# A two-layer graph network on one core: gathers, pair sums and loads placed in the time in which the first table is cleared

## The reference

```
h   = x mapped by lin1, times node_vec1            # 64 scalars, 32 vectors
w   = silu(edge_attr_64 @ fc_w1) @ fc_w2           # per-edge weights
es, ev = h_s[src], h_v[src]                        # gather of the source's row
m   = products of w, es, ev and edge_attr_4 (scalar, vector and cross products)
agg = segment_sum(m, dst)                          # scatter with addition
x1  = layernorm(x + gated(self_connection(x) + lin2(agg)))
```

## Time and profile before

| | us |
|---|---|
| median of 3 runs (lowest, highest) | 2219.08 (2218.88, 2225.33) |
| the profiled execution, its own time | 2213.97 |
| its span in the trace | 2212.2 |
| first layer, edges: start to the last scatter's landing | 0 to 767.7 |
| of that, up to the first scatter | 119.5 |
| first layer, nodes | to about 1170 |
| second layer, edges, with its start | to about 1920 |
| second layer, nodes | to 2212.2 |

### The profile page before, as it was taken

How to read it: one execution, slowest core, us unless ns; L and a number is a source line. 1 busy time by engine, 2 the same in 40 slices (tenths; PEclk the granted TensorE clock), 3 DMA queues, 4 the chain that set the end, 5 groups by cost and what they waited for, 6 DMA issues and landing times.

```text
span 2212.2 us, 47355 instructions
## 1 busy us (share of the span) xinstructions
PE 1427.5 (65%) x10302; PEld 1309.2 (59%) x10302; DVE 1478.8 (67%) x5824; ACT 1079.7 (49%) x3532; POOL 1507.3 (68%) x2020
## 2 busy tenths in 40 slices
PE   2098888888888566666655998888888888100000
PEld 2087777777777366566554987888888888000000
DVE  3087777777777188888883766555565565188886
ACT  1054444444444157767775545444454454066666
POOL 3067888778787456666664677777777776388876
PEclk7599999999999788999987999999999999555555
DMA  9956666666666578888874776676766776599996
GB/s 388 405 109 139 135 139 135 135 136 134 132 137 145 106 215 260 266 263 267 265 238 148 167 170 159 156 154 155 156 153 162 155 161 132 132 330 354 353 356 251
DMA packets 267990, 439.88 MB, mean 199 GB/s; under 512 B 34992, under 2 KB 145264, under 8 KB 264688
## 3 DMA queue, kind: packets, MB, share of 16 engines
q1 hardware_dynamic: 164400, 306.89, 43.2%
q0 software_dynamic: 75264, 67.79, 22.1%
q10 hardware_dynamic: 28224, 64.24, 7.7%
HBM read 235.50 MB, written 203.27 MB: 198 GB/s over the span
## 4 chain that ended last, share of the span: by engine, by line
POOL 28%; DMA 22%; issue 19%; PE 13%; DVE 6%; ACT 5%; SPq 4%; ACTq 1%; POOLq 0%; DVEq 0%
POOL table L459 13%; DMA table<-sums,row_all 9%; DMA tab<-table 7%; POOL xg L442 7%; DMA xg<-x_rows,src_all 3%; POOL half_rstd L495 3%; SPq L348 3%; DVE res L991 3%; ACT y L788 3%; DMA attrT<-in_attrT 3%; DVE stats L1000 2%; PE ps L590 1%; POOL gate L517 1%; PE ps L628 1%; PE ps L576 1%
## 5 line engine op out<-in xcount | busy, mean ns | idle before, releaser
L459 POOL DMA_INDIRECT table<-sums,row_all x392 | 631.3, 1610 | 351.5 <-ACT sums L742 161.8
L788 ACT ACTIVATE y<-res,shift,rstd 128x160 f32<-128x160 f32 x784 | 343.1, 508 | 233.4 <-POOL rstd L498 193.5
L727 ACT COPY msg<-ps 128x192 f32<-128x192 f32 (+1 forms) x196 | 57.4, 293 | 546.1 <-PE ps L609 541.0
L442 POOL DMA_INDIRECT xg<-in_x_rows,src_all x196 | 201.9, 1030 | 59.6 <-issue 58.4
L442 POOL DMA_INDIRECT xg<-x_rows,src_all x196 | 195.6, 998 | 68.2 <-issue 58.8
L934 DVE SCALAR_TENSOR_TENSOR x1g<-ps,a_all,x1g 128x160 f32<-128x160 f32 x392 | 132.5, 379 | 151.5 <-PE ps L629 151.2
L1000 DVE BATCH_NORM_STATS2 stats<-res 128x6 f32<-128x160 f32 x784 | 195.6, 311 | 4.6
L853 DVE TENSOR_TENSOR prod<-hs,ea_all 128x192 f32<-128x192 f32 x196 | 69.9, 357 | 190.2 <-ACT hs L702 187.9
L889 DVE TENSOR_TENSOR pe<-ps,ea_all 128x192 f32<-128x192 f32 x196 | 70.1, 358 | 166.6 <-ACT msg L727 134.0
L495 POOL TENSOR_TENSOR half_rstd<-var,minus_half 128x8 f32<-128x8 f32 x98 | 167.3, 1707 | 14.0
L590 PE MATMUL ps<-weights,midT 128*128 128x128 f32 (+1 forms) x784 | 165.4, 295 | 15.4 <-DVE msg L894 15.0
(11 more groups left out here) (114 smaller groups left out, 4782.0 us busy)
## 6 DMA issues: line engine op xcount, KB each, us to landing
tab<-table SPq DMA_DIRECT2D x98, 384.0 KB, 3.8
table<-zeros SPq DMA_DIRECT2D x24, 1536.0 KB, 37.4
table<-zeros SPq DMA_DIRECT2D x98, 324.0 KB
tab<-table SPq DMA_DIRECT2D x98, 324.0 KB, 5.1
x_rows<-y ACTq DMA_DIRECT2D x98, 320.0 KB, 3.1
x1g<-x_rows SPq DMA_DIRECT2D x98, 320.0 KB
base_rows<-x1g SPq DMA_DIRECT2D x98, 320.0 KB, 2.7
x1g<-base_rows SPq DMA_DIRECT2D x98, 320.0 KB, 4.8
```

Of the source, the lines that this page charges most:

```text
L442: pool.indirect_dma_start(out=xg[j % RING][:, t, 0:width], out_offset=None, in_=rows, in_offset=bass.IndirectOffsetOnAxis(ap=src_all[:, at ...
L459: pool.indirect_dma_start(out=table[l], out_offset=bass.IndirectOffsetOnAxis(ap=row_all[:, at:at + 1], axis=0), in_=sums[j % 4][:, t, 0:W] ...
L788: last = nc.scalar.activation(y[u][:, t, :], res[u][:, t, :], ACT.Identity, scale=rstd[u][:, t:t + 1], bias=shift[u][:, t:t + 1])
```

## The change

GpSimd's list in the first layer's edge part becomes: gathers of pairs 0 to 41, scatters of pairs 0 to 29, then in turn gather j+12 and scatter j for j = 30 to 85, then scatters 86 to 97. The gathers of pairs 0 to 33 (`EARLY`) write into the memory of `x1g` and `tab`, those of 34 to 41 into the eight `xg` buffers. A gather from pair 8 on waits, among the first 42, only until the gather of eight pairs before has landed. The sums of pairs 0 to 18 (`EARLY_SUMS`) are put into the memory of `res` and `y`, so that ScalarE needn't wait for a scatter before pair 23. The loads of edge scalars and destinations get rings of eight. SP issues eight of the 25 clearing DMAs behind the loads of pair 7 and the other 17 between the loads of pairs 8 to 19, one and two in turn; the clearing of the second table trails by 26 steps in place of 8. The first 34 steps are written out on each engine, in place of 10. The second layer changes only in its larger rings.

```diff
+EARLY, EARLY_SUMS = 34, 19
+AHEAD, BURST = EARLY + 8, 30
...
-        attrT = four("attrT", [P, P])
-        dst_row = four("dst_row", [P, PAIR], I32)
+        attrT = eight("attrT", [P, P])
+        dst_row = eight("dst_row", [P, PAIR], I32)
...
+        early_xg = (parts(x1g_all[:, :, :, :].rearrange("p u t c -> p (u t c)"), D + 1) +
+                    parts(tab_all[:, :, :, :].rearrange("p h g c -> p (h g c)"), D + 1))
+        early_sums = (parts(res_all[:, :, :, :].rearrange("p u t c -> p (u t c)"), 192) +
+                      parts(y_all[:, :, :, :].rearrange("p u t c -> p (u t c)"), 192))
...
                 def load_attr(j, m, u):
 
-                    wait_count(sp, s_hid, j - 3)
+                    wait_count(sp, s_hid, j - 7)
...
                 def load_dst_row(j, m, u):
 
-                    wait_count(sp, s_same, j - 3)
+                    wait_count(sp, s_same, j - 7)
...
                 def clear_table0(j, m, u):
-                    if isinstance(m, int) and m == 3:
+
+                    if not isinstance(m, int) or not RING - 1 <= m < EARLY:
+                        return
+                    if m == RING - 1:
                         sp.wait_ge(s_fill, 1)
...
+                    done = 0 if m == RING - 1 else RING + (m - RING) * 3 // 2
+                    for k in range(done, min(25, RING + (m - RING + 1) * 3 // 2)):
...
-                run_stages(sp, base, NP, 10, [(0, load_attr), (0, load_dst_row)] +
-                           ([(0, clear_table0), (8, clear_table1)] if l == 0 else [(4, store_base), (0, load_x1)]), RING)
+                run_stages(sp, base, NP, 10 if l else 26, [(0, load_attr), (0, load_dst_row)] +
+                           ([(0, clear_table0), (26, clear_table1)] if l == 0 else [(4, store_base), (0, load_x1)]), RING, 10 if l else EARLY)
...
                 def gather(j):
 
-                    wait_count(pool, s_xgT, j - RING + 1)
-                    if l == 0:
-                        wait_count(pool, s_ea, j - RING + 1)
+                    if l == 1 or j >= AHEAD:
+                        wait_count(pool, s_xgT, j - RING + 1)
+                        if l == 0:
+                            pool.wait_ge(s_ea, j - RING + 1)
+                    elif j >= RING:
+                        pool.wait_ge(s_gather[j % RING], landed(j - RING, j % RING, RING, 32))
...
-                for k in range(l * NP, (l + 1) * NP + RING):
-                    if k < (l + 1) * NP:
-                        gather(k)
-                    if k - RING >= l * NP:
-                        scatter(k - RING)
+                first, last = l * NP, (l + 1) * NP
+                ahead, burst = (RING, 0) if l else (AHEAD, BURST)
+                for j in range(first, first + ahead):
+                    gather(j)
+                for j in range(first, first + burst):
+                    scatter(j)
+                for j in range(first + burst, last):
+                    if j - burst + ahead < last:
+                        gather(j - burst + ahead)
+                    scatter(j)
...
                 def copy_sums(j, m, u):
 
                     act.wait_ge(s_sum, j + 1)
-                    wait_count(act, s_scat[u % 4], landed(j - 4, u % 4, 4, 32))
-                    copy(sums[u][:, :, 0:W], sum_ps[l][:, :, :]).then_inc(s_sumsb, 1)
+                    if not (isinstance(j, int) and j < EARLY_SUMS + 4):
+                        act.wait_ge(s_scat[u % 4], landed(j - 4, u % 4, 4, 32))
+                    copy(sums_of(j, u)[:, :, 0:W], sum_ps[l][:, :, :]).then_inc(s_sumsb, 1)
```

More of the change, by code:

```diff
@@ L53, in wait_count, with run_stages @@
         eng.wait_ge(sem, n)
-def run_stages(eng, base, count, depth, stages, unroll=4):
-    assert (count - depth) % unroll == 0
-    for k in range(base, base + depth):
+def run_stages(eng, base, count, depth, stages, unroll=4, lead=None):
+    lead = lead or depth
+    assert (count - lead) % unroll == 0
+    for k in range(base, base + lead):
         for lag, f in stages:
@@ L179, in program @@
         zT = four("zT", [T * V, P])
-        x1g = eight("x1g", [P, T, D])
+        x1g_all = sb("x1g", [P, RING, T, D])
+        x1g = [x1g_all[:, u, :, :] for u in range(RING)]
         x1z = two("x1z", [P, T, V])
         z1T = four("z1T", [P, 2, P])
-        tab2 = [sb(f"tab{h}", [P, 2, T * 192]) for h in range(RING // 2)]
+        tab_all = sb("tab", [P, RING // 2, 2, T * 192])
+        tab2 = [tab_all[:, h, :, :] for h in range(RING // 2)]
         tab = [tab2[u // 2][:, u % 2, :].rearrange("p (t c) -> p t c", t=T) for u in range(RING)]
         gate = two("gate", [P, T, 96])
-        res = eight("res", [P, T, D])
+        res_all = sb("res", [P, RING, T, D])
+        res = [res_all[:, u, :, :] for u in range(RING)]
         stats2 = [sb(f"stats{h}", [P, 2, T, 6]) for h in range(RING // 2)]
@@ L194, in program, with parts, xg_of, sums_of @@
         shift = [shift2[u // 2][:, u % 2 * T:(u % 2 + 1) * T] for u in range(RING)]
-        y = four("y", [P, T, D])
+        y_all = sb("y", [P, 4, T, D])
+        y = [y_all[:, u % 4, :, :] for u in range(RING)]
+        def parts(flat, width):
+            n = flat.shape[1] // (2 * width)
+            cut = flat[:, 0:n * 2 * width].rearrange("p (n t c) -> p n t c", n=n, t=2)
+            return [cut[:, k, :, :] for k in range(n)]
+        early_xg = (parts(x1g_all[:, :, :, :].rearrange("p u t c -> p (u t c)"), D + 1) +
+                    parts(tab_all[:, :, :, :].rearrange("p h g c -> p (h g c)"), D + 1))
+        early_sums = (parts(res_all[:, :, :, :].rearrange("p u t c -> p (u t c)"), 192) +
+                      parts(y_all[:, :, :, :].rearrange("p u t c -> p (u t c)"), 192))
+        assert len(early_xg) >= EARLY and len(early_sums) >= EARLY_SUMS
+        def xg_of(j, u):
+            return early_xg[j] if isinstance(j, int) and j < EARLY else xg[u]
+        def sums_of(j, u):
+            return early_sums[j] if isinstance(j, int) and j < EARLY_SUMS else sums[u % 4]
         small2 = [sb(f"small{h}", [P, 4, 2, T]) for h in range(RING // 2)]
@@ L235, in program @@
         s_src = sem("src_loaded")
-        s_attr = sem4("attr_loaded")
-        s_drow = sem4("dst_row_loaded")
+        s_attr = [sem(f"attr_loaded{u}") for u in range(RING)]
+        s_drow = [sem(f"dst_row_loaded{u}") for u in range(RING)]
         s_gather = [sem(f"rows_gathered{u}") for u in range(RING)]
@@ L442, in gather @@
                         pool.indirect_dma_start(
-                            out=xg[j % RING][:, t, 0:width], out_offset=None, in_=rows,
+                            out=xg_of(j, j % RING)[:, t, 0:width], out_offset=None, in_=rows,
                             in_offset=bass.IndirectOffsetOnAxis(ap=src_all[:, at:at + 1], axis=0)).then_inc(s_gather[j % RING], 16)
@@ L806, in _ @@
             nc.vector.memset(zeros[:, :], 0.0).then_inc(s_fill, 1)
+            for u in range(RING):
+                nc.vector.memset(attr1T[u][:, :], 0.0)
             for u in range(4):
-                nc.vector.memset(attr1T[u][:, :], 0.0)
                 nc.vector.memset(z1T[u][:, :, :], 0.0)
```

33 lines of the change are left out of this document (16 added, 17 removed).

## The result

The changed kernel takes 2239.93 us (2238.43 to 2245.53, 5 runs) beside 2219.08 us (2213.70 to 2225.33, 5 runs) for the kernel before: the ratio is 1.0097, with a 95% interval of 1.0077 to 1.0117. It is about 21 us slower, where 3 us less had been forecast, and outside the range. The profiled executions have spans of 2238.1 and 2212.2 us; these are 25.9 us apart and not 21, as the profiled execution before lies 5 us under the median.

The account below looks back on a forecast made before the run. It took full DMA to bound the edge part up to the first scatter, then GpSimd's loop, with scatter landings just underneath. A start 10.1 us later minus 12.9 us of faster scatters gave -2.8 us: 2216.3 us, range 2203 to 2231.

Parts of the forecast that it names:

- The loop at 6.62: First layer's edge part: 56 scatter intervals with gathers keep 6.62 us each, 370.7 us; SP's longer lag costs zero.
- the second limit: Edge loop: each scatter waits for the previous landing, so removing two gathers saves only 0.23 to 0.5 us a period.
- The start: First layer's scatter 0: starts at 129.6 us instead of 119.49, losing 10.1 us, behind the clearing and gather 41.
- Gathers: Under the clearing: 27 more pairs landed, 0.43 us each, delay its end by 11.6 us (9.9 to 15.6).
- Loads: Ahead of the last clearing DMA: sixteen more pairs at 0.57 us, 9.1 us, plus 1 us for SP's issue.
- The gathers' landing: Gathers ahead of scatter 0: at most 3.38 us a pair, so gather 41 is out at 126.2.
- rival B: Gathers become the bound at 4.1 us a pair; scatter 0 at 142, total 2228.7 us; chance 0.21.
- bare periods: Scatters without gathers between them: 29 intervals at 6.3 us each, 182.7 us together.
- the last twelve: Final bare scatter intervals up to scatter 97: 25.6 us, 8.3 over a clearing burst, and 42.7.
- Rival A: Clearing hardly pays for loads and gathers, ending near 122; 16 to 18 us faster, 2202; chance 0.29.
- Rival C: Bare scatters no faster, landing stretched to 3.1 us by loads and pieces; 2224 us; chance 0.13 with Rival D.
- Rival D: List misbehaves, for instance TensorE held back after its rest, loop 30 to 85 slower; 5 us and more, counted in Rival C.

Follow-up runs that it names:

- a_sync: The changed kernel, but in SP's written loop the second table's clearing piece waits for scatter k-12 instead of k-26; 2222.89 us, ratio 1.0036 to the kernel before.
- v_gather: v_eight with the changed kernel's 42 pairs of gathers ahead and 30 scatters in a row; 2214.49 us, ratio 0.9990 to the kernel before.
- v_eight: The kernel before with load rings of eight and the first table's whole clearing behind pair 7's loads instead of pair 3's; 2209.30 us, ratio 0.9959.
- v_eight_again: The same kernel as v_eight, timed in more rounds on another occasion, against the kernel before; 2210.56 us, ratio 0.9955.
- v_six: v_eight with the first table's clearing behind pair 5's loads instead of pair 7's; 2207.53 us, ratio 0.9947 to the kernel before.
- b_nogather: The kernel before without the first layer's gathers from pair 8 on, so results are wrong; loop period 6.35 us instead of 6.64, one run 2194.47 us.
- v_lag26: v_eight with the second table's clearing piece waiting for scatter k-26 instead of k-8, 34 SP steps written out; 2291.51 us, ratio 1.0373.
- v_lag26_noclear: v_lag26 with the second table's clearing pieces moved into one burst behind the last loads; loop period 7.03 us, total 2289.45 us.
- b_noclear1: The kernel before with the second table's clearing pieces moved into one burst behind the last loads; loop period 6.54 us instead of 6.64, one run 2253.52 us.

## Why the prediction was wrong

*The loop at 6.62, wrong.* This is the step that failed outright: 18.4 of the 21.4 us that the pace was short of the forecast. The prediction looked at SP's longer lag only for whether loads would come too late, and put "zero". They came early enough; what the lag took away was the moment of issue. With SP held by landings (a_sync, v_gather) the loop is 6.61 and 6.58. That the landing was the second limit, 0.23 us under the loop, stood two paragraphs earlier, and so did the share of pieces and loads in the traffic; what was missing was that anything which moves those transfers against the scatter moves the period.

*The start, mis-sized in two terms.* Scatter 0 came 137.15 - 107.6 = 29.6 us behind the mark of the kernel before, where 21.7 had been forecast for the clearing. Gathers: 0.43 us a pair was right (0.45 and 0.46), but all 33 more pairs went inside the clearing, not 27: 14.9 us in place of 11.6. (The prediction's upper case and the expectation of v_gather count 34.)

Loads: the rest, 14.6 us in place of 9.1 + 1. It is 3.7 us for the first four pairs (v_eight, 111.34 - 107.6; 3.3 by v_eight_again), and 10.9 us between v_gather and after. For the second part here are packets and SP's queue, first of v_gather from 122 us to its scatter 0 and from 0 to 122, then of after from 133 us to its scatter 0 and from 0 to 133:

```profile
DMA packets 534, 0.74 MB, mean 174 GB/s; under 512 B 125, under 2 KB 440, under 8 KB 534
...
q1 hardware_dynamic: 6603, 42.31, 84.8%
```

```profile
DMA packets 756, 0.60 MB, mean 145 GB/s; under 512 B 84, under 2 KB 742, under 8 KB 756
...
q1 hardware_dynamic: 10936, 45.33, 85.5%
```

Behind 122 and 133 us every packet is under 8 KB, so the clearing's rows of 12 KB are all through. Up to these marks, 11 us apart, SP's queue moved 3.02 MB more in after. At 0.197 MB a pair of loads that is about 15 pairs, not 12, and its packets took 113.7 - 103.5 = 10.2 us more: 0.67 us a pair, just within the prediction's bound of 0.68. So two things were missed. The middle of 0.46 and 0.68 was taken, and the loads of some three pairs that stand behind the last clearing piece in SP's list were carried ahead of its last rows, so a load that is written behind the clearing isn't always transferred behind it. From 130 us to scatter 0, only nine of 1681 packets are of 8 KB or more: this is the thin tail. It isn't after's own cost, since in v_gather, too, the last 4.2 us ahead of scatter 0 have no row of the clearing. From 133 us on after moves loads alone, 0.60 MB with 54.6% of 4.15 us: 0.74 us a pair, so the excess over their bytes' 0.46 does not need the clearing beside them. The 0.92 us a pair that the expectation of v_six works with counts twelve pairs where fifteen went.

*The gathers' landing, wrong.* Rows of the first three pairs were read as a pace of 3.38 us; GpSimd issued all 84 gathers at 1.25 us with no wait, the last at 108.90, and scatter 0 waited 27.31 us for the clearing alone. So rival B had the right sign for the wrong reason. The rule that the Trainium skill gives in "DMA: Bandwidth & Descriptors", section "Queues, rings and completion order" (queues take turns packet by packet), was applied with four packets of a gather per engine, which gave 4.1 us a pair. The trace of after holds 4032 packets on GpSimd's queue for 84 gathers, three per gather and engine if all engines have the same share, which by that rule is an estimate of 2.8 us a pair with 0.46 us per clearing packet. At an issue of 2.5 us no gather had to wait for the one of eight pairs before, which allows for a lag, so no run here tells whether the rule held them.

```profile
q0 software_dynamic: 4032, 6.93, 14.1%
```

*Right:* bare periods (6.38 for 6.3), the last twelve (77.3 for 76.6), the second limit (b_nogather 6.35), TensorE's rest without harm, no effect on the later parts.

*Rival A* was wrong, the clearing paid in full. *Rival C* had named a landing stretched by loads and pieces, but for the bare scatters; it came in the loop. *Rival D* had named a slower loop, by 5 us and more, but with TensorE held back as its reason. None of the signs that the prediction gave for being wrong came: scatter 0 lies between 122 and 139 and the bare periods between 6.1 and 6.6, for there was no sign on the loop with gathers.

*Left open:* why a pair of loads takes 0.67 us and more of DMA time where its bytes would take 0.46; why VectorE's use, and with it the piece, falls badly in two periods of eight in after and in nearly all of v_lag26. That the loads, and not the loops' jump, make the remaining 0.39 us of v_lag26_noclear is an inference from what is left.

## What to carry to other kernels

In a chain of DMAs that wait for each other's landing, the moment at which other queues issue can matter more than how much they issue: here the pieces cost 0.10 us a period behind a landing (b_noclear1), and letting SP loose cost 1.08 (v_lag26). Hold them by the same landing, and when a wait is loosened, ask what it had been timing. Work that is moved into a stretch where DMA is full costs its whole DMA time there, so it must save more than that later; here gathers ahead cost 0.45 us a pair and saved 0.3 to 0.4. Before buying a whole stretch of hidden compute, count what the next engine needs first: six to eight pairs of early loads brought the first scatter 8 to 10 us forward, and 33 more pairs of gathers and 19 parked sums gave nothing more.

## What the runs showed of the hardware that was not expected

When a pair's scatter (two indirect DMAs with addition) is followed 2 to 3 us after its start by a 324 KB store and 192 KB of loads from another queue, the period to the next scatter is 1.0 to 1.5 us longer than with the same transfers issued 1 us ahead of it (v_lag26 against v_eight; in after 1.3 to 1.4). Loads of 64 KB in rows of 512 bytes and 128 KB in rows of 1 KB took 0.67 us of DMA time a pair beside a clearing and 0.74 by themselves, where their bytes at 429 GB/s would take 0.46. Loads that SP issued behind a clearing piece were carried ahead of its last rows, three pairs of them. GpSimd's gathers kept their issue pace of 1.25 us beside a clearing at 410 GB/s.
